# A mixture-of-experts stage with routed rows: expert numbers read in one go, plain f32 down products in one chunk, a table SiLU, a larger descriptor ring

## The reference

```python
for e in range(2):                      # shared experts, hidden 256 each
    h = silu(x @ s_w1[e].T) * (x @ s_w3[e].T)
    shared += h @ s_w2[e].T
s = sigmoid(concat([x, t_emb]) @ W_router.T)      # 8 experts
_, idx = top_k(s + bias, 2)
gates = chosen s / (sum of chosen s)
for e in range(8):                      # routed experts, hidden 128 each
    routed += gelu(x @ r_w1[e].T) @ r_w2[e].T * gates[:, e]
cond = (shared / 2 + routed) / 4        # then layer 0's second part:
# expert-choice feed-forward on cond: scores, softmax, top 8 tokens per
# sequence and expert, gather, gelu(x @ w1) @ w2, scatter-add, residual
```

## Time and profile before

| | us |
|---|---|
| median of 3 runs | 600.64 |
| lowest, highest | 598.59, 602.14 |
| the profiled execution, its own time | 601.76 |
| its span in the trace | 600.4 |
| PE busy | 541.9 (90%) |
| DVE busy | 449.3 (75%) |
| ACT busy | 362.8 (60%) |
| POOL busy | 198.4 (33%) |

### The profile page before, as it was taken

One profiled execution on the slowest core, in us unless ns is written; L12 is line 12 of the kernel. 1 busy time (PEld: TensorE's weight loads), 2 busy tenths in 40 slices (PEclk: granted clock), 3 DMA queues, 4 the chain that ended last, 5 costly groups with the idle time before them and its releaser, 6 DMA issues.

```text
span 600.4 us, 10472 instructions
## 1 busy us (share of the span) xinstructions
PE 541.9 (90%) x3332; PEld 467.1 (78%) x3332; DVE 449.3 (75%) x1151; ACT 362.8 (60%) x824; POOL 198.4 (33%) x200
## 2 busy tenths in 40 slices
PE   8999988998476788879899998998999999999997
PEld 7877866776366677778799897877899899998786
DVE  5978578588434236859978644898999899999966
ACT  5567745554212244355635333698898888889975
POOL 5688856756500026659545000001000000100100
PEclk9999997999678699989999999999999999999998
DMA  8623950362186651130030000002001111112121
GB/s 287 189 106 149 389 163 0 101 203 76 44 256 171 174 178 48 48 110 5 1 125 4 0 1 1 1 19 37 19 20 36 19 28 27 28 26 38 44 62 37
DMA packets 50118, 49.05 MB, mean 82 GB/s; under 512 B 23232, under 2 KB 42720, under 8 KB 49504
## 3 DMA queue, kind: packets, MB, share of 16 engines
q1 hardware_dynamic: 48016, 44.05, 24.9%
q0 software_dynamic: 2048, 4.33, 2.3%
HBM read 37.08 MB, written 10.69 MB: 80 GB/s over the span
## 4 chain that ended last, share of the span: by engine, by line
PE 56%; DVE 16%; POOL 9%; issue 8%; SPq 4%; DMA 3%; ACT 3%; DVEq 0%; ACTq 0%; POOLq 0%
PE bank L1685 6%; POOL routed_x L816 5%; PE bank L368 4%; PE bank L370 4%; PE bank L2124 4%; PE bank L369 4%; PE bank L2210 4%; PE bank L2114 4%; PE bank L2151 3%; PE bank L2152 3%; POOL y_rows L992 3%; DVE scat L1810 2%; PE bank L1755 2%; SPq L824 2%; SPq L825 1%
## 5 line engine op out<-in xcount | busy, mean ns | idle before, releaser
L2505 POOL CAST h_high<-h 128x256 fp32r<-128x256 f32 x15 | 6.4, 426 | 198.9 <-ACT h L2316 192.6
L992 POOL DMA_INDIRECT y_rows<-routed_y,slot_at x32 | 32.0, 1000 | 75.3 <-DMA routed_y<-y_out 57.9
L368 PE MATMUL bank<-xin_high,sw_high 128*128 128x256 f32 x128 | 43.6, 340 | 5.6 <-DVE sw_low L1658 3.3
L2151 PE MATMUL bank<-taps_high,q1T 128*128 128x512 f32 x94 | 43.0, 458 | 1.0 <-ACT q1T L2279 0.6
L816 POOL DMA_INDIRECT routed_x<-x_rows,slot_at x32 | 32.6, 1019 | 18.8 <-issue 18.8
L1685 PE MATMUL bank<-th,w 128*128 128x256 f32 x128 | 33.8, 388 | 4.2 <-DVE topf L1527 3.2
L2152 PE MATMUL bank<-taps_low,q1T 128*128 128x512 f32 x94 | 37.1, 395 | 0.0
L422 POOL TENSOR_TENSOR hidden_low<-hidden,hidden_high 128x512 fp32r<-128x512 f32 x24 | 31.1, 1301 | 16.6 <-ACT hidden_high L417 16.4
L2114 PE MATMUL bank<-x,lstm_wx 128*128 128x128 f32 x256 | 34.4, 277 | 1.7 <-ACT gates_t L2252 0.9
L369 PE MATMUL bank<-xin_low,sw_high 128*128 128x256 f32 x128 | 35.7, 279 | 0.0
L370 PE MATMUL bank<-xin_high,sw_low 128*128 128x256 f32 x128 | 35.7, 279 | 0.0
(11 more groups left out here) (322 smaller groups left out, 1838.3 us busy)
## 6 DMA issues: line engine op xcount, KB each, us to landing
big<-gates_scratch SPq DMA_DIRECT2D x3, 2048.0 KB, 7.2
w_ring<-routed_w SPq DMA_DIRECT2D x39, 132.0 KB, 2.9
w<-in_f_w SPq DMA_DIRECT2D x16, 256.0 KB
onehot<-topi_scratch SPq DMA_DIRECT2D x8, 512.0 KB
routed_y<-y_out SPq DMA_DIRECT2D x13, 204.0 KB, 2.5
xs<-routed_x SPq DMA_DIRECT2D x13, 192.0 KB, 3.1
outT<-x SPq DMA_DIRECT2D x15, 128.0 KB, 2.0
xT<-in_xT SPq DMA_DIRECT2D x3, 512.0 KB, 7.5
```

The costliest lines, as they stand in the source:

```text
L368: pe.matmul(dst, wh[:, cols], vh[:, :], start=start, stop=False)
L992: pool.indirect_dma_start(y_rows[c % 2][:, r, i, :], None, ys_dram[:, :], bass.IndirectOffsetOnAxis(slot_at[:, r, tile:tile + 1], 0)).then ...
L2151: pe.matmul(dst, q, taps_high[:, 2 - j, :], start=True, stop=False)
```

## The change

1. Sparse stage: SP reads all 39 expert numbers into registers in one go ahead of the first weight transfer, and the weight transfers use these registers. The stores of y stay on SP.
2. The ring for indirect transfers is 4096 bytes instead of 1024.
3. Chunk 3 (`WHOLE`): the down products are one plain f32 matmul each, from `hidden` and unsplit down weights (`whole_sw2`, `whole_rw2`) that SP loads at the end of chunk 2. ACT's high and POOL's low parts of that chunk's 12 units go; a factor of 1/16 for the shared units moves into DVE's product. `hidden` is now freed by the down product.
4. Shared chunks: ACT applies the table function Silu instead of Tanh, and DVE makes `hidden` in one operation instead of two.
5. Slot work, `chunk_*` pieces and the choice move to other units; the choice for chunks 0 to 3 is made one chunk earlier. `load_gate_rows(3, 1)` is issued behind four other transfers instead of ahead of them.
6. `y_rows` lie in the memory of the taps (two full buffers), so POOL's first write of `taps_high` waits for the last `combine`. `y_stored` rounds up: for m = 12 it now waits for 7 stores of the even buffer instead of 6.

```diff
@@ load_raw_weights
-                sp.wait_ge(s_hi, ALL_UNITS)
-                sp.wait_ge(s_lo, ALL_UNITS)
+                sp.wait_ge(s_hi, ALL_SPLIT)
+                sp.wait_ge(s_lo, ALL_SPLIT)
@@ prepare_weights
+                    if k == 0:
+                        pool.wait_ge(s_comb, 2 * (NCHUNK - DENSE))
                     pool_p(pool.tensor_copy(taps_high[:, k, :], tap))
@@ hidden_free
-                if not (below(c, 1) and u < 3):
+                if c == WHOLE and u >= 3:
+                    dve.wait_ge(s_down, c * NUNITS + (u - 2))
+                elif not (below(c, 1) and u < 3):
                     dve.wait_ge(s_lo, c * NUNITS + (u - 2))
@@ second_product
+                if c == WHOLE:
+                    if u == 0:
+                        pe.wait_ge(s_gw, WHOLE_READY)
+                    if kind == "sh":
+                        pe.wait_ge(s_q, c * NSH + j + 1)
+                    else:
+                        pe.wait_ge(s_gg, c * NRO + j + 1)
+                    w = whole_sw2 if kind == "sh" else whole_rw2
+                    pe.matmul(acc_bank[par][:, :], w[:, j * P:(j + 1) * P], hidden[u % 3][:, :],
+                              start=u == 0, stop=u == NUNITS - 1).then_inc(s_down, 1)
+                    return
@@ chunk
-                for u in range(n):
-                    hidden_low(c, u)
-                    if u == 6:
-                        x_low(c + 1, 1 - par)
+                if c < WHOLE:
+                    for u in range(n):
+                        hidden_low(c, u)
+                        if u == 6:
+                            x_low(c + 1, 1 - par)
+                else:
+                    x_low(c + 1, 1 - par)
...
                 if c == 2:
-                    load_gate_rows(3, 1)
                     sp.dma_start(x_rows[:, :], t["x_rows"]).then_inc(s_rows, 16)
...
+                    load_gate_rows(3, 1)
                 if c == 3:
                     sp.wait_ge(s_gg, 3 * NRO)
+                    sp.dma_start(whole_sw2, t["s_w2T"]).then_inc(s_gw, 16)
+                    sp.dma_start(whole_rw2, t["r_w2T"]).then_inc(s_gw, 16)
+                    sp.wait_ge(s_gw, WHOLE_READY)
                     sp.dma_start(rw2_rows, t["r_w2"]).then_inc(s_gw, 16)
@@ shared_tanh, shared_silu
-                act.activation(th[k % 2][:, :], shared_pair(k)[0][:, :], ACT.Tanh, scale=0.5).then_inc(s_th, 1)
+                act.activation(th[k % 2][:, :], shared_pair(k)[0][:, :], ACT.Silu).then_inc(s_th, 1)
@@ shared_silu, shared_hidden
-                dve.scalar_tensor_tensor(pb[k % 2][:, :], th[k % 2][:, :], 1.0, shared_pair(k)[0][:, :],
-                                         ALU.add, ALU.mult).then_inc(s_p, 1)
-                dve.wait_ge(s_p, k + 1)
...
-                dve.tensor_tensor(hidden[v % 3][:, :], pb[k % 2][:, :], shared_pair(k)[1][:, :], ALU.mult).then_inc(s_q, 1)
+                dve.scalar_tensor_tensor(hidden[v % 3][:, :], th[k % 2][:, :], 2.0, shared_pair(k)[1][:, :],
+                                         ALU.mult, ALU.mult).then_inc(s_q, 1)
@@ load_weights
-                    e = sp.value_load(tile_expert[0:1, k:k + 1], min_val=0, max_val=E - 1)
-                    sp.dma_start(w_ring[k % (RING * TRIO)], wcat[ds(e, 1), :, :].rearrange("o p k -> (o p) k")
+                    sp.dma_start(w_ring[k % (RING * TRIO)], wcat[ds(tile_experts[k], 1), :, :].rearrange("o p k -> (o p) k")
@@ y_stored
-                    eng.wait_ge(s_yst[k], 16 * ((m + 1 - k) // 2))
+                    eng.wait_ge(s_yst[k], 16 * ((m + 2 - k) // 2))
@@ shared_sp
+                for k in range(SPARSE_TILES):
+                    tile_experts.append(sp.value_load(tile_expert[0:1, k:k + 1], min_val=0, max_val=E - 1))
                 for m in range(RING):
                     load_weights(m)
@@ kernel
-    nc = bacc.Bacc("TRN2", target_bir_lowering=False, num_devices=1, dynamic_dma_scratch_size=1024)
+    nc = bacc.Bacc("TRN2", target_bir_lowering=False, num_devices=1, dynamic_dma_scratch_size=4096)
```

More of the change, by code:

```diff
@@ L297, in build_program @@
             den, dpos = sb0("den", [P, NTILE, 1]), sb0("dpos", [P, NTILE, 1])
-            assert nc.sbuf_base - at_route == 4 * 2 * TILES_CHUNK * YROW
-            y_rows = [sb0("y_rows0", [P, 2, TILES_CHUNK, YROW]),
-                      nc.alloc_sbuf_tensor_at("y_rows1", [P, 2, TILES_CHUNK, YROW], F32, offset=at_route)]
+            y_rows = [nc.alloc_sbuf_tensor_at(f"y_rows{k}", [P, 2, TILES_CHUNK, YROW], F32, offset=at_taps + k * 4 * 3 * HT * P)
+                      for k in range(2)]
             slot_at = sb0("slot_at", [P, 2, HALF], U32)
@@ L495, in shared_on_vector @@
                 hidden_free(c, u)
-                dve.tensor_tensor(hidden[u % 3][:, :], pb[j % 2][:, :], ab_bank[j % 2][1][:, :], ALU.mult).then_inc(s_q, 1)
+                if c < WHOLE:
+                    dve.tensor_tensor(hidden[u % 3][:, :], pb[j % 2][:, :], ab_bank[j % 2][1][:, :], ALU.mult).then_inc(s_q, 1)
+                else:
+                    dve.scalar_tensor_tensor(hidden[u % 3][:, :], pb[j % 2][:, :], 1.0 / 16.0, ab_bank[j % 2][1][:, :],
+                                             ALU.mult, ALU.mult).then_inc(s_q, 1)
             def routed_gelu(c, j):
@@ L569, in chunk @@
                         chunk_store_scores(c - 1, 1 - par)
-                    if c == 2 and u == 11:
+                    if c == 3 and u == 0:
                         slots_counted()
-                    if c == 3 and u == 0:
+                    if c == 3 and u == 1:
                         slots_based()
-                    if c == 3 and u == 1:
+                    if c == 3 and u == 2:
                         slots_placed()
-                    if c == 3 and u == 3:
-                        slots_gated()
                     if c == 3 and u == 4:
+                        slots_gated(0)
+                    if c == 3 and u == 7:
+                        slots_gated(1)
+                    if c == 3 and u == 10:
                         slots_experts()
@@ L654, in slots_placed, with slots_gated @@
                 dve.tensor_copy(slot_at[:, :, :], pair_at).then_inc(s_sided, 1)
[L656 to L662, removed]
+            def slots_gated(r):
+                at = pair_at[:, r, :].rearrange("p (i o) -> p i o", o=1).to_broadcast([P, HALF, E])
+                dve_pos(dve.tensor_tensor(by_tile(equal), by_tile(placed), at, ALU.is_equal))
+                dve_pos(dve.tensor_tensor(by_tile(equal), by_tile(equal), gates[:, HALF:NTILE, :], ALU.mult))
+                dve_pos(dve.tensor_reduce(slot_gate[:, r, :], by_tile(equal), X, ALU.add))
             def slots_experts():
@@ L714, in shared_down @@
                     pe.wait_ge(s_sided, GATE_WEIGHTS)
-                if c == NCHUNK - 1 and j == 0:
+                if c == CHOICE_CHUNK + 2 and j == 0:
                     pe.wait_ge(s_dc, TURNED)
@@ L794, in shared_dve @@
                         shared_x_low(c + 1)
-                    if j == 0 and c > DENSE:
-                        chunk_store_scores(c - 2, c % 2)
-                    if c == CHOICE_CHUNK - 1 and j == 1:
+                    if j == 2:
+                        chunk_store_tokens(c - 1, 1 - c % 2)
+                    if j == 3:
+                        chunk_store_scores(c - 1, 1 - c % 2)
+                    if c == CHOICE_CHUNK and j == 0:
                         choice_scores(0)
-                    if c == CHOICE_CHUNK - 1 and j == 3:
+                    if c == CHOICE_CHUNK and j == 2:
                         choice_probs(0)
-                    if c == CHOICE_CHUNK + 1 and j == 0:
-                        choice_tables(0, acc_bank[c % 2][:, P:2 * P], (0, 1))
-                    if c == CHOICE_CHUNK + 1 and j == 1:
+                    if c == CHOICE_CHUNK + 1 and j == 3:
+                        choice_tables(0, acc_bank[1 - c % 2][:, P:2 * P], (0, 1))
+                    if c == CHOICE_CHUNK + 2 and j == 0:
                         choice_tables(0, None, (2, 3))
                         choice_rows(0)
-                    if j == NSH - 1:
-                        chunk_store_tokens(c - 1, 1 - c % 2)
                 shared_low(LAST_SHARED - 1)
-                chunk_store_scores(NCHUNK - 2, NCHUNK % 2)
             def scatter_pool():
```

51 lines of the change are left out of this document (31 added, 20 removed).

## The result

| | us |
|---|---|
| after, median of 4 runs | 560.19 (559.17 to 566.92) |
| before, median of 4 runs beside it | 600.77 (598.59 to 602.14) |
| ratio | 0.9351, 95% interval 0.9273 to 0.943 |
| the same two kernels once more, 5 runs of after | 560.60, ratio 0.9339, 0.9309 to 0.9368 |
| after's profiled execution, its own time; its span | 560.55; 559.2 |

The time lies under it: the direction was right and the sum too small by 11 us. Busy times by stretch: chunk 3, the shared chunks, the sparse stage with its ends, the groups (the same 95 us as in the earlier trace rows), and, as the last line, the sparse stage cut as in the earlier trace rows, from the first rows asked for to the last weights landed. The columns are the stretch, its length, PE, PEld, DVE, ACT and POOL, PE's clock, the busy share of the transfer engines, GB/s.

What follows compares the result with a forecast made beforehand. SP's list was taken to bound the sparse stage. A start 18.9 us earlier and 11.8 from the loop made 30.7; with +0.9 and -0.7 behind it, 30.5 off 601.76 gave 571 us, range 562 to 582.

Steps and rivals of the forecast that it cites:

- the ring's term: Gathers after the sparse stage: larger ring saves about 4 us of gaps, but DVE waits only 0.73 us: -0.7 us.
- Behind it: From the sparse loop's end onward: tail unchanged, +0.9 us for the rounded store wait, -0.7 us for the ring.
- The loop's term: Sparse loop: SP's blocks fall from 4.59 to 2.9 us, last weights landed at 181, 11.8 us won.
- Chunk 3, end at 109.2: Chunk 3 in plain f32: last down product ends at 109.2 instead of 115.25, 6.0 us earlier.
- The scatter: POOL's scatter starts at about 90 and is over by 136, so the larger ring is worth nothing here.
- The 39 reads: SP's list before the sparse loop: 39 reads at 0.57 us take 22.2 us, from 112.1.
- The allowance of 2.1 us for a disturbed list: SP's list before the first xs: a quarter of 8.2 us for disturbed reads and transfers, first xs at 145.3.
- The shared chunks: Shared chunks: with DVE's chain shorter they take 36 us, so PE is done at 145 instead of 159.
- The tail from there to the first gather: From last weights landed to POOL's first gather: 8.8 us stays, plus 0.9 us for the last store.
- faster than the sum: Rival on the sparse stage: SP undisturbed, PE at full clock, blocks overlapping, 564 us; chance 0.14.
- Transfers bound the loop: Rival on the sparse loop: transfers set its pace and it wins nothing, 583 us; chance 0.10.
- The slower ones: Rivals: SP's list slower than taken, about 579 us, chance 0.14; PE's clock at its lower level, about 628 us, 0.02.

Runs made afterwards that it cites:

- the repeat: The kernel before, unchanged, run once more for a second trace: 599.33 us.
- the four versions beyond: The kernel after with nine expert reads moved ahead: alone 558.34 us; with y stores on ACT 559.28; with three y_out buffers 557.90; with both 558.03.
- three more edits: Nine expert reads moved ahead, y stores on ACT, three y_out buffers, on the kernel after: lowest median 557.90 us, with the first and third.

## Why the prediction was wrong

**The step that failed is the ring's term in the part "Behind it"**: "DVE waits for it only 0.73 us: -0.7". Undoing the ring in the kernel after costs 4.8 us in that part and 3.5 us in all; on the kernel before, a ring without stalls in the gathers wins 3.8 to 6.6 us there, by which of its two traces one takes. The loop's term, below, was too small by nearly as much (3.7 us), but by sizes alone; here the way of pricing was wrong. A wait that an engine shows for a resource is what the resource is late beyond the engine's own lateness, in that one execution. In the first trace DVE had been held up for 3 us, which did not recur and most likely hid the rest; the repeat showed 3.26. The chain of waits had both stalls on the path, and a piece of PE at half clock behind them. A sum of 2.06 + 2.20 - 0.60 = 3.7 us from two rows of that chain would have come close, and with the clock's share, 2.04 us against the 0.86 that the same four records take at 262.98 in the same chain, it comes to 4.8. That it meets the 4.8 of the undoing so exactly is in part luck: there the stalls were 3.2 us of it, the later landing 1.4 us, and part of what the low clock cost went into a wait of 1.04 us that PE has in the kernel after.

Point by point, in the sum of 30.5 us against 41.2 measured on the spans (one slip lies outside the sum: the 571 starts from the profiled execution, 1.1 us above the median; from the median it would be 570):

- Chunk 3, end at 109.2: the last two records begin at 108.86, so 109.7. Right, and so was 0.86 us a down product. Gate weights 107.82 (107.2), first read 112.59 (112.1): right.
- The scatter from 88.73 to 132.1 (90 to 136), one stall of 2.37 us: right. That "the larger ring is worth nothing" here holds in the kernel after, where the scatter is over long before SP is (with 1024 it ends at 135.4, and the first xs stay at 143.10); on the kernel before it was worth 5.4 us.
- The 39 reads: 112.59 to 135.26, 22.7 us (22.2), median 267 ns, and 15 weight transfers in 7.95 (8.0):

```profile
L888 SPq TENSOR_LOAD <-tile_expert x39: 260/267/459, 112.6 to 134.6; - x39
```

  The allowance of 2.1 us for a disturbed list was too much: first xs at 144.27 (145.3). Its source, the 1.40 us a pair, did not recur in the repeat (1.11). The Trainium skill's floor of about 600 ns for a `tensor_load` (DMA: Bandwidth & Descriptors, Latency and other measured facts) is again not what this trace shows; by it the time would have missed by 13 us more.
- The shared chunks, where DVE loses one operation of three per unit and PE was to be done at 145: it is done at 147.5. The first work of the sparse stage follows at once, 1.3 us before the 148.8 of the sum. But the table SiLU is worth 3.4 us of the total, since PE's end, not SP's list alone, sets the start. I had named SP as the only one.
- The loop: last weights landed at 177.3 instead of the 181 of the sum, the second term that was mis-sized, by 3.7 us. 1.0 of it is the start. SP's pitch of 2.9 was right (2.95), but a block lost 2.0 us by the change, not 1.7, as the run with the reads in the loop shows as well: 2.1 us over eight blocks. The last transfer took 3.5 us to land instead of 2.29. And I had added 1.6 us because I let the transfers' 33.0 us of full work run at 0.93 busy. They ran at 0.97: from the first xs to the last landing 33.0 us passed, 32.0 of them full work. So the work was estimated nearly right, and the idle share put too high.
- The tail from there to the first gather: 186.72 - 177.3 = 9.4 us, where 8.8 + 0.9 stood. Right to 0.3 us.
- Behind the first gather: 7.4 instead of 0.7. Of that the ring is 4.6 to 4.8, as shown; the other 2.8 are the profiled execution of the kernel before, whose repeat had 377.1.

The pieces are 3.7 + 0.3 + 6.7 = 10.7 us. Of the rivals "faster than the sum" was the right one with the wrong parts: its full clock came true, its 564 was still too cautious because the ring was not in it. "Transfers bound the loop" is near the truth as a limit (a share of 0.96 to 1.06 in the four versions beyond) and false as a loss. The slower ones did not occur.

Taken singly, undoing an edit costs against 560.60: chunk 3 13.8 us, reads 13.1, ring 3.5, SiLU 3.4. These add up to 33.8 of 39.8 us. The ring alone on the kernel before gave 11.6, since there it also moves the scatter, which later the plain products cover; single undoings need not add up to the whole. The moves of point 5 of the change (slot work, `chunk_*` pieces, the choice a chunk earlier) were undone in no run, so what they are worth stays open.

## What to carry to other kernels

Price a removed stall by the chain of waits, not by the wait that one engine shows for it: the engine's own lateness hides part of it, and that lateness may be a chance of the one execution traced. A second trace of the kernel before would have told it, and would have spared the allowance for SP's burst too. When an edit frees an engine (here POOL, 22 us earlier), look at what that engine does next, for that was worth more than the edit's own place. When SP's list has been shortened to where PE's own work ends, the next limit is a microsecond away: three more edits there gave 2.7 us at most.

## What the runs showed that I had not expected

- A descriptor ring of 2048 bytes let 32 gathers in a row pass without a stall, where 1024 gave four of 2.1 to 3.5 us each, in both kernels, ahead of the 8th, 16th, 24th and 32nd gather. In the scatter, 4096 still left one (2.37 us), 2048 two, 1024 four, ahead of the 8th, 15th, 22nd and 29th transfer.
- The ring takes room from the kernel's own buffers: on the kernel before 4096 did not fit beside them.
- Two traces of one unchanged kernel, 0.4 us apart in span, differed by 3.2 us in the place of the first gather and by 2.8 us in what came behind it. A part of a span is less sure than the whole.
- The share of the transfer engines reached 1.06 at 329 GB/s in a stretch of 24 us, where the kernel after had 1.00 at 300, so a share near 1.00 does not yet mean that not one byte more would go through.
